# A centering matrix moved from a VectorE step into the loaded table of constants

## The reference

```
x_in = x @ w_in;  dt = softplus(...) * 0.099 + 0.001;  A = -exp(A_log)
step:  h = exp(dt * A) * h + inp_term          # 16 states for each of 128 channels, over 1024 tokens
       y = sum over states of h * c + Dp * u
x = x + y
logits = layernorm(x) @ Wr + br                # router: 128 channels to 8 experts
```

## Time and profile before

| | us |
|---|---|
| median of 3 runs | 458.99 |
| lowest and highest run | 456.33, 459.06 |
| span of the profiled execution | 493.5 |

### The profile page before, as it was taken

One profiled execution on the slowest core, in us unless ns is written; L12 is line 12 of the kernel. 1 busy time (PEld: TensorE's weight loads), 2 busy tenths in 40 slices (PEclk: granted clock), 3 DMA queues, 4 the chain that ended last, 5 costly groups with the idle time before them and its releaser, 6 DMA issues.

```text
span 493.5 us, 5720 instructions
## 1 busy us (share of the span) xinstructions
PE 372.6 (75%) x1686; PEld 187.6 (38%) x1686; DVE 341.5 (69%) x770; ACT 240.5 (49%) x396; POOL 285.0 (58%) x196
## 2 busy tenths in 40 slices
PE   4889753676886977888439988885899878598692
PEld 3334310312412412424214355444566766244341
DVE  4898899999999999986220366763569855145341
ACT  2787835256556556626032338633687211336440
POOL 2142369699999999943724000178536665316764
PEclk9999955698788788799959999996789896579996
DMA  7114240872100100100302114211201121122201
GB/s 209 21 73 130 55 127 0 292 266 76 44 0 2 42 1 1 42 0 18 99 22 87 51 40 135 86 53 43 76 1 44 44 82 60 40 93 94 61 14 31
DMA packets 28555, 32.78 MB, mean 66 GB/s; under 512 B 5213, under 2 KB 20593, under 8 KB 28524
## 3 DMA queue, kind: packets, MB, share of 16 engines
q1 hardware_dynamic: 24268, 25.40, 16.6%
q0 software_dynamic: 3456, 6.31, 4.2%
q10 hardware_dynamic: 800, 0.71, 0.5%
HBM read 13.91 MB, written 19.38 MB: 67 GB/s over the span
## 4 chain that ended last, share of the span: by engine, by line
PE 37%; DVE 24%; issue 17%; ACT 9%; another core or an unknown queue 7%; POOL 3%; DVEq 2%; ACTq 1%; DMA 0%
DVE states L706 15%; PE ps L1539 5%; PE ps L1550 4%; PE ps L1758 3%; POOL states L851 2%; PE ps L1271 2%; PE ps L1003 2%; ACT scaled L1319 2%; PE ps L1859 2%; PE ps L1118 2%; PE ps L1542 2%; PE ps L1262 1%; PE ps L151 1%; PE ps L1844 1%
## 5 line engine op out<-in xcount | busy, mean ns | idle before, releaser
L851 POOL TENSOR_TENSOR states<-states,c_rows 128x1024 f32<-128x1024 f32 x60 | 143.5, 2427 | 18.9 <-DVE states L706 18.6
L706 DVE TENSOR_TENSOR_SCAN states<-ps,inp 128x1024 f32<-128x1024 f32 x64 | 140.5, 2259 | 0.2 <-issue 0.2
L700 ACT ACTIVATE ps<-ps,bias_p,scale_p 128x1024 f32<-128x1024 f32 x64 | 75.0, 1177 | 66.0 <-PE ps L694 65.9
L1092 POOL DMA_INDIRECT slots<-x,put x52 | 50.7, 975 | 49.1 <-DVE put L1086 35.2
L694 PE MATMUL ps<-stack,sel 96*128 96x512 bf16 x128 | 47.7, 466 | 40.2 <-DVE states L706 40.0
L1215 POOL DMA_INDIRECT x<-answers,put x24 | 23.6, 984 | 58.9 <-DMA answers<-reply 52.0
L1414 POOL DMA_INDIRECT out<-reply,home x32 | 31.8, 993 | 27.1 <-DVE reply L1391 19.1
L1391 DVE SCALAR_TENSOR_TENSOR reply<-ps,rows,kept 128x128 f32<-128x128 f32 x64 | 18.6, 344 | 30.7 <-PE ps L1271 19.4
L694 PEld LDWEIGHTS ps<-stack,sel 96*128 96x128 bf16 x128 | 9.1, 104 | 77.7 <-DVE states L706 71.3
L1508 ACT ACTIVATE d_hidden<-ps,b 128x512 f32<-128x512 f32 x24 | 16.4, 685 | 42.7 <-PE ps L1542 35.7
L728 PE MATMUL ps<-states,red 128*32 128x512 f32 x256 | 36.7, 679 | 0.2 <-POOL states L851 0.2
(11 more groups left out here) (199 smaller groups left out, 700.2 us busy)
## 6 DMA issues: line engine op xcount, KB each, us to landing
slots<-zero SPq DMA_DIRECT2D x8, 528.0 KB
rows<-slots SPq DMA_DIRECT2D x16, 264.0 KB
steps<-part SPq DMA_DIRECT2D x4, 768.0 KB, 3.3
stack<-steps SPq DMA_DIRECT2D x12, 256.0 KB, 4.2
answers<-x SPq DMA_DIRECT2D x4, 512.0 KB, 3.2
answers<-reply SPq DMA_DIRECT2D x8, 256.0 KB, 2.5
x<-in_x SPq DMA_DIRECT2D x3, 512.0 KB, 6.6
out<-x SPq DMA_DIRECT2D x3, 512.0 KB
```

The source lines that it names most:

```text
L700: act.activation(bank(ps, slot(b, u), 2), bank(ps, slot(b, u), 2), ACT.Exp, scale=m["scale_p"][:, group(u):group(u) + 1], bias=m["bias_p"] ...
L706: dve.tensor_tensor_scan(h[:, u * SEQ:(u + 1) * SEQ], bank(ps, slot(b, u), 2), inp[:, b * SEQ:(b + 1) * SEQ], 0.0, ALU.mult, ALU.add).then ...
L851: eng.tensor_tensor(h[:, u * SEQ:(u + 1) * SEQ], h[:, u * SEQ:(u + 1) * SEQ], c_rows[:, b * SEQ:(b + 1) * SEQ], ALU.mult).then_inc(done, 1)
L1092: pool.indirect_dma_start(out=m["slots"][n // BATCH], out_offset=bass.IndirectOffsetOnAxis(m["put"][:, b, i:i + 1], 0), in_=m["x"][:, b * ...
```

## The change

The table gets 128 more columns, `C_CENTER`, filled on the host with the centering matrix. The second part of the table's load grows from 968 to 1096 columns. The tile `center`, the step that made it and its semaphore `centered` go. `router_weights` reads the table's columns and waits for `consts_in` in place of `centered`.

```diff
-C_END = C_SLOT + TILES
+C_CENTER = C_SLOT + TILES
+C_END = C_CENTER + P
...
+    t[:, C_CENTER:C_CENTER + P] = np.eye(P) - 1.0 / D
...
-             "center": plan.sb("center", [P, P]),
...
+    m["consts_in"] = consts_in
...
-    scanned, prod_dve, centered = plan.sems("vector", "scanned prod_dve centered")
+    scanned, prod_dve = plan.sems("vector", "scanned prod_dve")
...
-            need(pe, centered, 1)
+            pe.wait_ge(m["consts_in"], 16)
             pe.wait_ge(m["router_in"], 16 * 2)
-            pe.matmul(ps[:, 7 * HALF:7 * HALF + EXPERTS], m["center"][:, :], m["w_r_raw"][:, :], start=True, stop=True).then_inc(weight_psum, 1)
+            pe.matmul(ps[:, 7 * HALF:7 * HALF + EXPERTS], const[:, C_CENTER:C_CENTER + P], m["w_r_raw"][:, :], start=True, stop=True).then_inc(weight_psum, 1)
...
-                if b == 0 and u == 9:
-
-                    dve.tensor_scalar(m["center"][:, :], ident, -1.0 / D, None, ALU.add).then_inc(centered, 1)
```

## The result

The changed kernel takes 454.31 us (median of 20 runs), the kernel before 456.32 us (median of 20, the first three of them those shown above, which lay high). The ratio is 0.9949, with a 95% interval from 0.9932 to 0.9965: 0.51% of 456.32, or 2.3 us; the two medians differ by 2.0. The forecast was a gain of 2.27 us, within 1% of the kernel before, at 456.7 us. The gain came as forecast.

A forecast was written before the change was run, and what follows sets the result against it. The prediction took DVE to pace the scan, with no slack at the centering step. Its one large term, 2.27 us, gave 458.99 - 2.27 = 456.7 us; the range was 453.7 to 460.2 us.

The forecast's parts named there:

- The step goes, 2.27 us: Centering step leaves DVE in row 0 of the scan; what follows starts 2.27 us sooner, bounds 0.14 and 2.36.
- The next scans are not held: DVE's scans of units 9 and 10 have their decays ready and are not held by POOL's product of unit 8.
- the hold that passes on: Rival: the scan of unit 9 waits for POOL's product as the step did; only 0.14 us won, 458.9 us, chance 0.12.
- GpSimd's wait shrinks to 2.27: POOL's wait ahead of its product of unit 10 in row 0 falls from 4.54 to 2.27 us.
- DVE's product of unit 9: It meets POOL's product of unit 10 as before, both released by the scan of unit 10; nothing added.
- The router's matmul: On PE it no longer waits 4.23 us for DVE, starting near 84.0; costs nothing, gains nothing.
- a new wait for bank 7: The router's matmul writes PSUM bank 7 earlier; the forecast was no new wait.
- The table's load: Load ahead of the scan grows from 484 to 548 KB; cost 0, bound 0.3 us, under a cover of 1.1 us.
- The clock rivals: PE's clock changes fall elsewhere behind the scan: slower, 462.0 us, chance 0.08, or faster, 451.5 us, chance 0.07.

The follow-up runs named there:

- e2: Changed kernel with the centering step put back at its old place on VectorE, twice in a row: steps 2.36 and 0.21 us, scan length 143.55 us, ratio 1.0101.
- e3: Changed kernel with the step put back but reading PSUM instead of SBUF: step 0.28 us, scan length 141.30 us, ratio 0.9924.
- e4: Kernel before, old table, with the step moved ahead of the scans where GpSimd has nothing to do: step 0.22 us, scan length 141.11 us, ratio 0.9950.
- e1: Changed kernel with the step put back at its old place, into a tile nobody reads: step 2.36 us, scan length 143.46 us, ratio 1.0078.
- e9: Changed kernel with 256 more unread table columns, 676 KB: load landed 4.9 us after issue, DVE waited 0.18 us, scan length 141.23 us, ratio 0.9878.
- e6: Changed kernel with VectorE's last third_part moved between the scan of unit 10 and VectorE's product of unit 9: scan length 142.20 us, ratio 0.9960.
- e5: Changed kernel with GpSimd's first product waiting for VectorE's three leftovers behind the first scan: scan length 138.93 us, ratio 0.9889, median 451.98 us.
- e8: Changed kernel with GpSimd waiting twice, ahead of its first product and its product of unit 7: scan length 137.46 us, ratio 0.9794.
- e0: Kernel before, unchanged, timed against itself: step 2.36 us, scan length 143.51 us, ratio 1.0019.
- e7: Changed kernel with the edits of e5 and e6 together: scan length 139.29 us, ratio 0.9919.

## Why the prediction was right

Point by point, in its own numbering:

1. *The step goes, 2.27 us.* Right in size and cause. The scan length shrinks by 143.49 - 141.20 = 2.29 us, and the timed gain is 2.3 us. The reading of the step as a turn in a queue for SBUF is shown, not only argued: 0.21 us right behind a product (e2), 0.28 from PSUM beside one (e3), 0.22 ahead of the scans (e4).
2. *The next scans are not held.* Right: 4.46 us for two, at 85.44, while GpSimd's product runs to 87.72. The rival of the hold that passes on is refuted by this row and by e3. The comparison of 2.19 with 2.23 us a scan was no evidence, though: these are averages over 16 and over 2 scans that overlap by 0.08 us, and singly a scan takes 2.26 to 2.29 in either case.
3. *GpSimd's wait shrinks to 2.27.* It is 2.26.
4. *DVE's product of unit 9.* 1.19 us, as before.
5. and 6. *The router's matmul* starts at 83.43, forecast near 84.0; PE waits for DVE behind it. It costs and brings nothing in the scan (e1, e4). No trace shows a new wait for bank 7.
7. *The table's load.* There is no wait at DVE's first read. Its bound of 0.3 us is about what the landing takes longer over all traces, a median of 3.7 us against 3.5, and it stayed under the cover; e9 finds the edge of the cover.

The clock rivals didn't show in the median. One run in 20, the one of 490.96 us, did have a much lower granted clock, 0.705, but there is no trace of it, so whether that is what the rival meant is open. Over the other 19 runs of the changed kernel, 452.8 to 457.3 us, the mean granted clock doesn't follow the time (a correlation of -0.06). No trace of the kernel before is free of the unknown waits, so its stretch behind the scan can't be set against the changed kernel's.

Two things in the prediction were less good than they look. The time, 456.7, was taken from a median of three runs that lay 2.7 us above the median of twenty; the difference was right and its base was not. So 454.31 lies outside the band from 455.5 to 458.2 that was given 0.73, and just under the 454.4 that was to mean "faster"; it is within 1% of the kernel before only because that one's median fell too, and the range only just left room for it (453.7). That the time landed in the range is in part luck. And the prediction left the profiled execution's 34.5 us on top unexplained. They were inside it, behind the scan, in waits that the profile page of the kernel before names in the shares of its chain, a line that I had not weighed:

```profile
PE 37%; DVE 24%; issue 17%; ACT 9%; another core or an unknown queue 7%; POOL 3%; DVEq 2%; ACTq 1%; DMA 0%
```

The chain has seven such waits, 34.4 us in sum. Against the median of twenty the excess is 37 us, so they are most of it and not exactly all. Nothing in the sum hung on that, because its one term lies in the scan.

## What to carry to other kernels

When a short VectorE instruction takes many times its usual duration, compare its end with the end of GpSimd's instruction beside it; if they coincide, as here, the price is the turn, and removing it, moving it to where GpSimd is idle, or reading from PSUM gave back about the same (2.29, 2.38 and 2.19 us of scan length). Moving a held instruction next to another VectorE instruction of that kind only moved the turn (e6); letting GpSimd stand still, where it has slack, takes it away (2.27 us for one line in e5). Work off VectorE's path is worth its held duration, not its work, as long as VectorE is what the next engine waits for.

## What the runs showed of the hardware that I had not expected

- The two engines take turns. In e6 GpSimd's product was waiting when third_part ended at 88.3, and went ahead of the VectorE product that followed directly; in e8 VectorE's product was waiting when GpSimd's product of unit 8 ended, and went ahead of GpSimd's next. In both cases the one that was waiting at the end of the turn was next, though the other engine had an instruction ready. It had also started to wait first (87.27 against 88.23 in e6, 86.48 against 86.86 in e8), so a rule of taking turns and one of first come, first served can't be told apart here.
- On three of the chips this single-core kernel took 7 to 9% more by the medians (the kernel before 493.4 to 497.3 us against 456.9, the changed one 487.7 against 454.3), all of it behind the scan, where the traces have six to ten waits of 1.4 to 8.3 us with no releaser. In e0 the chain has eight of them, 45.0 us in sum:

```profile
233.68 6.92 another core or an unknown queue
245.82 6.76 another core or an unknown queue
327.04 7.49 another core or an unknown queue
```

The traces of the changed kernel and of e4 to e7 have none. They went with the set of runs and its chip. What causes them wasn't found.
